# A three-part network on one core: a token mixer whose engines take some hundred pieces per chunk in a written order of their own

## The reference

```python
delta = shifted - x
z = tanh((x + delta * mu_x) @ W_x1.T)                   # 5 x 32 low-rank channels
mus = einsum('blnr,dnr->blnd', z, W_x2) + x_bias        # five mixes of 256 channels
r = (x + delta * r_mu) @ W_r.T                          # k, v, g alike, w by two matmuls
w = tanh((x + delta * w_mu) @ A_w.T) @ B_w.T + b_w
# per token: o = q (S + u k v), S = exp(-exp(w)) S + k v
o = (o - mean) / sqrt(var + EPS) * gn_weight + gn_bias
y = (o * silu(g)) @ W_o.T
```

## Time and profile before

| | us |
|---|---|
| median of 3 executions (3580.39 to 3586.51) | 3586.17 |
| the profiled execution | 3589.31 |
| its span in the trace | 3587.5 |
| mixer, first 16 chunks' work to its last residual add | 0 to 874.9 |
| PE, DVE, ACT, POOL busy over the whole span | 92%, 69%, 56%, 22% |
| granted TensorE clock, whole span | 0.935 |

### The profile page before, as it was taken

How to read it: one execution, slowest core, us unless ns; L and a number is a source line. 1 busy time by engine, 2 the same in 40 slices (tenths; PEclk the granted TensorE clock), 3 DMA queues, 4 the chain that set the end, 5 groups by cost and what they waited for, 6 DMA issues and landing times. The chain is left out here.

```text
span 3587.5 us, 77850 instructions
## 1 busy us (share of the span) xinstructions
PE 3299.5 (92%) x31396; PEld 1943.6 (54%) x31396; DVE 2487.4 (69%) x4742; ACT 2006.8 (56%) x2999; POOL 775.6 (22%) x888
## 2 busy tenths in 40 slices
PE   7999999995899939999999999999999999987998
PEld 3555556554677814444444444444444444436777
DVE  5766676664777717777868778677687776826776
ACT  2444444442555503666766667666666666675555
POOL 2444444442222210102011011020110201011222
PEclk8898888886899966999999999999999999998999
DMA  1000000002111142121212222131212212102111
GB/s 49 14 25 13 25 25 25 14 14 67 61 48 48 36 95 38 27 43 46 43 30 59 41 48 42 23 66 25 58 34 38 54 35 39 38 13 85 48 54 36
DMA packets 110294, 145.48 MB, mean 41 GB/s; under 512 B 21616, under 2 KB 94208, under 8 KB 109152
## 3 DMA queue, kind: packets, MB, share of 16 engines
q1 hardware_dynamic: 109168, 137.69, 16.3%
q0 software_dynamic: 768, 2.82, 0.4%
HBM read 53.89 MB, written 38.24 MB: 26 GB/s over the span
## 5 line engine op out<-in xcount | busy, mean ns | idle before, releaser
L1795 DVE TENSOR_REDUCE b_half_max<-banks 128x1 f32<-128x512 f32 x2048 | 1314.6, 685 | 443.5 <-PE banks L1520 262.3
L1746 ACT ACTIVATE b_p_t<-banks 128x1024 f32<-128x1024 f32 x1024 | 1045.8, 1024 | 398.3 <-PE banks L1520 256.7
L1576 PE MATMUL banks<-b_k_stack,b_q_stack 62*128 62x512 f32 x2048 | 828.5, 477 | 34.1 <-issue 17.8
L1637 PE MATMUL banks<-b_q_stack,b_k_stack 64*128 64x512 f32 x2048 | 851.5, 469 | 0.0
L1592 PE MATMUL banks<-b_p_t,b_v 128*17 128x256 f32 x8192 | 640.9, 385 | 25.1 <-ACT b_pv L1715 24.5
L1637 PEld LDWEIGHTS banks<-b_q_stack,b_k_stack 64*128 64x128 f32 x2048 | 343.0, 185 | 432.1 <-issue 416.7
L1520 PE MATMUL banks<-b_tables,b_halves 64*128 64x128 bf16 x4096 | 437.0, 224 | 0.0
L1576 PEld LDWEIGHTS banks<-b_k_stack,b_q_stack 62*128 62x128 f32 x2048 | 337.6, 188 | 68.5 <-issue 24.9
L1125 ACT ACTIVATE ffn_relu<-banks,ffn_scale_fc 128x512 f32<-128x512 f32 x256 | 176.0, 687 | 234.1 <-PE banks L1057 234.0
L1070 PE MATMUL banks<-ffn_proj_t,ffn_r_hi 128*128 128x256 f32 x1024 | 262.2, 289 | 8.7 <-DVE ffn_r_lo L1251 8.7
L1592 PEld LDWEIGHTS banks<-b_p_t,b_v 128*17 128x17 f32 x8192 | 136.0, 95 | 225.1 <-issue 77.0
(11 more groups left out here) (232 smaller groups left out, 4978.2 us busy)
## 6 DMA issues: line engine op xcount, KB each, us to landing
ffn_x<-x SPq DMA_DIRECT2D x32, 512.0 KB, 3.9
b_q_stack<-b_qk_hi SPq DMA_DIRECT2D x256, 64.0 KB
b_k_stack<-b_qk_hi SPq DMA_DIRECT2D x256, 64.0 KB
a_x<-hidden_states SPq DMA_DIRECT2D x16, 512.0 KB, 4.1
x<-a_x SPq DMA_DIRECT2D x16, 512.0 KB, 2.9
x<-ffn_x SPq DMA_DIRECT2D x16, 512.0 KB, 2.8
b_x<-x SPq DMA_DIRECT2D x8, 1024.0 KB, 5.8
b_k_stack<-b_qk_lo SPq DMA_DIRECT2D x128, 64.0 KB
```

The costliest lines, as they stand in the source:

```text
L1576: last = pe.matmul(m, q_stack[rows, slot, qb * P:(qb + 1) * P], k_stack[rows, slot, half * BANK:(half + 1) * BANK], start=True, stop=not h ...
L1637: last = pe.matmul(out, k_stack[stack, slot, kb * P:(kb + 1) * P], q_stack[stack, slot, half * BANK:(half + 1) * BANK], start=True, stop=n ...
L1746: act.activation(p_t[use % P_BUFS][:, :, :], scores[use % 2], ACT.Exp, scale=slopes()[pair][0]).then_inc(p_made, 1)
L1795: dve.tensor_reduce(half_max[:, (pair + rg * PAIRS) * QB + qb, half:half + 1], misc.at["max", g, turn], axis=AX.X, op=ALU.max, negate=True ...
```

## The change

The four generators of each engine are cut into named pieces (`turn`, `mix_in`, `low`, `pair_products`, `carry_over`, `output`, `project_out`, `level` and so on), and `schedule` goes. Each engine has a list of its own for one turn, written out, with the chunk that each piece works on: PE's reaches from chunk `c - 2` to `c + 2`, DVE's to `c + 3`. `advance` is cut in `carry_over` and `output`, which can stand apart; the last block's `output` and the output projections of a chunk come one turn later than before, and `keys` now comes before `queries`. ACT's `queries`, `keys` and `take_values` get a wait of their own for the buffers (`used_up`), and the tree's first level one for `q`. No instruction, tile or buffer count of the computation changes.

```diff
@@ -221,8 +221,10 @@
         MIXED = ((0, 0), (1, 0), (0, 1), (1, 1), (2, 0), (3, 0), (2, 1), (3, 1), (4, 0), (4, 1))
         SCALED = [max(i for i, (j, _) in enumerate(MIXED) if j == mix) + 1 for mix in range(MIXES)]
         FIRSTS, WEIGHTS = 4, 6 + 1 + 6 + 4 + 2 * KT
-        NORMALIZE, PREPARE, RECUR, FINISH = 7, 14, 8, 12
         Z_ROWS = (P, 2 * LOWRANK)
+
+
+        TURNS = range(-3, CHUNKS + 3)
         ring = Ring([banks[:, i, :] for i in range(6)], (zeroed, 1))
         mix = lambda j: mixes[j % (MIXES - 1)]
 
@@ -232,6 +234,10 @@
         def mix_free(c, j):
 
             return ((g_ready, 2 * c), (r_ready, c), (k_ready, c), (v_ready, 2 * c), (low_ready, c + 1))[j]
+
+        def on(c, piece, *which):
+            if 0 <= c < CHUNKS:
+                piece(c, *which)
 
...
-        def schedule(recur, finish, prepare, normalize):
-            for c in range(-2, CHUNKS + 1):
-                side_by_side(*([(RECUR, recur(c), 1)] if 0 <= c < CHUNKS else []),
-                             *([(FINISH, finish(c - 1), 1)] if c > 0 else []),
-                             *([(PREPARE, prepare(c + 1), 1)] if 0 <= c + 1 < CHUNKS else []),
-                             *([(NORMALIZE, normalize(c + 2), 1)] if c + 2 < CHUNKS else []))
-                yield c
-
...
+            def carry_over(c, i):
+                t, keys = CT * c + i, k_tok[(CT * c + i) % 2]
+                b, (used, n) = ring.take(("kv", c, i), (state_made, t + 1))
+                pe.wait_ge(used, n)
+                pe.wait_ge(v_made, 2 * c + i // 2 + 1)
+                pe.wait_ge(k_tok_made, t + 1)
+                for h in range(HEADS_A):
+                    r = h * HK
+                    last = pe.matmul(b[r:r + HK, 0:HV], keys[:, r:r + HK], v[c % 2][:, i, h * HV:(h + 1) * HV],
+                                     start=True, stop=True, tile_position=(0, r))
+                last.then_inc(kv_ready, 1)
+
+            def output(c, i):
+                tok, t = i * P, CT * c + i
+                fresh, weights = t % QB == 0, pair[t % 2]
+                b, (used, n) = ring.take(("o", c, i), (o_made, t + 1))
+                pe.wait_ge(used, n)
+                if not fresh:
+                    pe.wait_ge(state_spread, t)
+                    pe.matmul(b[:, 0:VD], q_up[c % 2][TREE][:, tok:tok + P], spread_state[t % 2][:, :, :].rearrange("p h n -> p (h n)"),
+                              start=True, stop=False)
+                pe.wait_ge(near_placed, t + 1)
+                for h in range(HEADS_A):
+                    last = pe.matmul(b[:, h * HV:(h + 1) * HV], weights[:, h, :], v[c % 2][:, i, h * HV:(h + 1) * HV],
+                                     start=fresh, stop=fresh or h == HEADS_A - 1)
+                last.then_inc(o_ready, 1)
+
...
+            for c in TURNS:
+                on(c + 1, mix_in, 0)
+                on(c + 1, mix_in, 2)
+                on(c, pair_products, 0)
+                on(c - 1, output, 3)
+                on(c - 2, project_out, 0)
+                on(c - 2, project_out, 1)
+                on(c - 2, project_out, 2)
+                on(c + 1, mix_in, 4)
+                on(c + 1, mix_in, 6)
+                on(c + 1, low)
+                on(c, pair_products, 1)
+                on(c - 2, project_out, 3)
+                on(c + 1, decays)
+                on(c + 1, mix_in, 8)
+                on(c + 1, keys)
+                on(c, carry_over, 0)
+                on(c, pair_products, 2)
+                on(c, carry_over, 1)
+                on(c, output, 0)
+                on(c + 1, queries)
+                on(c + 2, turn, 0)
+                on(c, output, 1)
+                on(c + 2, turn, 1)
+                on(c + 1, values, 0)
+                on(c, pair_products, 3)
+                on(c, carry_over, 2)
+                on(c + 1, gates, 0)
+                on(c + 1, values, 1)
+                on(c - 1, turn_out)
+                on(c, output, 2)
+                on(c + 1, gates, 1)
+                on(c + 2, low_rank, 0)
+                on(c + 2, low_rank, 1)
+                on(c, carry_over, 3)
...
+            def decays(c):
+                dec = decay[c % 2]
                 act.wait_ge(w_ready, c + 1)
                 used_up(c - 2)
...
+            for c in TURNS:
+                on(c + 1, take_low_rank, 1)
+                on(c, level, 6)
+                on(c, pair_products, 0)
+                on(c - 1, output, 3)
+                on(c + 1, low)
+                on(c - 1, squares)
+                on(c, pair_products, 1)
+                on(c + 1, keys)
+                on(c + 1, decays)
+                on(c, pair_products, 2)
+                on(c, output, 0)
+                on(c + 1, queries)
+                on(c + 1, level, 0)
+                on(c, output, 1)
+                on(c + 2, take_turned, 0)
+                on(c + 1, level, 1)
+                on(c + 1, take_values, 0)
+                on(c + 1, level, 2)
+                on(c + 2, take_turned, 1)
+                on(c + 1, level, 3)
+                on(c, pair_products, 3)
+                on(c - 1, take_o_t, 0)
+                on(c + 1, take_values, 1)
+                on(c + 1, take_gates, 0)
+                on(c + 1, level, 4)
+                on(c + 1, take_gates, 1)
+                on(c, output, 2)
+                on(c + 1, level, 5)
+                on(c + 2, take_low_rank, 0)
+                on(c - 1, take_o_t, 1)
...
+            for c in TURNS:
+                on(c, pair_products, 0)
+                on(c - 2, project_out, 0)
+                on(c + 1, add_x)
+                on(c - 2, project_out, 1)
+                on(c - 2, project_out, 2)
+                on(c + 1, mix_in, 4)
+                on(c + 1, mix_in, 6)
+                on(c, pair_products, 1)
+                on(c - 2, project_out, 3)
+                on(c - 1, power)
+                on(c + 1, mix_in, 8)
+                on(c, carry_over, 0)
+                on(c + 2, normalize)
+                on(c, pair_products, 2)
+                on(c, carry_over, 1)
+                on(c - 1, scale)
+                on(c + 1, level, 0)
+                on(c + 1, level, 1)
+                on(c + 1, level, 2)
+                on(c, pair_products, 3)
+                on(c + 2, difference)
+                on(c, carry_over, 2)
+                on(c + 2, first_mix)
+                on(c + 1, level, 3)
+                on(c + 1, gates, 0)
+                on(c + 1, level, 4)
+                on(c + 3, moments_of)
+                on(c + 1, level, 5)
+                on(c + 1, level, 6)
+                on(c + 1, gates, 1)
+                on(c, carry_over, 3)
+                on(c + 2, mix_in, 0)
+                on(c + 2, mix_in, 2)
...
+            for c in TURNS:
+                on(c, level, 4)
+                on(c, level, 5)
+                on(c - 1, carry_over, 2)
+                on(c, level, 6)
+                on(c - 1, carry_over, 3)
+                on(c - 2, gate_out)
+                on(c + 2, root)
+                on(c + 1, add_x, 2)
+                on(c + 1, add_x, 3)
+                on(c + 2, carry_token)
+                on(c - 1, root_out)
+                on(c, carry_over, 0)
+                on(c + 1, level, 0)
+                on(c + 1, add_x, 4)
+                on(c + 1, level, 1)
+                on(c + 1, level, 2)
+                on(c, carry_over, 1)
+                on(c + 1, level, 3)
```

More of the change, by code:

```diff
@@ new lines, in values @@
+            def values(c, h):
+                b, (used, n) = ring.take(("v", c, h), (v_made, 2 * c + h + 1))
+                pe.wait_ge(used, n)
+                pe.wait_ge(*mixed(c, 3))
+                for i in range(2):
+                    tok = (2 * h + i) * P
+                    out = b[:, i * VD:(i + 1) * VD]
+                    pe.matmul(out, mix(3)[:, 0, tok:tok + P], w_v[:, 0, :], start=True, stop=False)
+                    last = pe.matmul(out, mix(3)[:, 1, tok:tok + P], w_v[:, 1, :], start=False, stop=True)
+                last.then_inc(v_ready, 1)
@@ L400, in recur @@
[L400 to L412 removed]
+                                out, moving = products[at:at + BLOCK, h, LEVEL[l]:LEVEL[l + 1]], qs[l][r, now]
@@ new lines, in pair_products @@
+                                if l:
+                                    out, moving = out.rearrange("p (n m) -> p n m", m=1 << l), upper(moving, l)
+                                pe.matmul(out, ks[l][r, now], moving, start=True, stop=True, tile_position=(h * HK, at))
+                    for at in range(0, P, BLOCK):
+                        late = tok + BLOCK + at // 2
+                        for h in heads:
+                            r = slice(h * HK, (h + 1) * HK)
+                            last = pe.matmul(products[at:at + BLOCK, h, LEVEL[NEARBY]:], ks[NEARBY][r, tok:tok + BLOCK],
+                                             qs[NEARBY][r, late:late + BLOCK // 2], start=True, stop=True, tile_position=(h * HK, at))
```

(43 more changed lines are left out.)

651 lines of the change are left out of this document (220 added, 431 removed).

## The result

The changed kernel takes **3489.67 us** (median of four runs, 3481.44 to 3500.58); before takes 3584.2 in the runs beside it. The ratio is 0.9739, with a 95% interval of 0.9703 to 0.9775: 94 us less. The forecast was 3490. Two of the four runs are near 3481, two near 3499.

A forecast was written before the change was run, and what follows sets the result against it. PE was taken to bound the kernel. Per chunk, 42.0 us of full-clock work + 0.5 of new wait + 2.0 of lost clock = 44.5 in place of 50.9; 96 us less over 15 chunks gave 3490 us, range 3450 to 3565.

The forecast's parts named there:

- The wait between pair products 0 and 1: PE's wait for `a_pair`, 1.6 us per chunk, goes because over 7 us of other work now stands there.
- The new wait: At the turn's start `mix_in` waits for the low-rank tanh: 0.5 us per chunk, counted in full.
- The other engines: DVE, ACT and POOL work, tree levels and `add_x` cost nothing while PE needs over 42 us per chunk.
- the ring: PE's waits for banks at `mix_in` 4 to 7 and `low`: taken as 0, bounds 0 and 1 us per chunk.
- Four `mix_in` as one issue: At the turn's start, four matmuls on two row groups run at once, in one issue of 1.06 us.
- rival B: `mix_in` goes two by two, 2.1 us, with a clock fall each chunk: 47.6 us per chunk, 3537 us; chance 0.23.
- The 42.0 us of PE work at full clock: PE's work per chunk, from the old 50.9 us less 6.4 of half clock and 2.5 idle.
- The clock: Falls to half speed every second chunk, 8 us each: 4 us per chunk, costing 2 us; bounds 0 and 6.4.
- Ends: First and last turns: 1 us more, up to 8 us more and up to 4 us less; taken as 0.
- Rival A: The clock never falls in the mixer's turns: 42.5 us per chunk, 126 us less, 3460 us; chance 0.30.
- Rival C: The clock falls twice a turn, at the start and pair products 2: 52.5 us per chunk, 3610 us; chance 0.07.

The follow-up runs named there:

- control: The changed kernel again, unaltered, measured beside the follow-ups: 3483.15 us.
- gates_last: Changed kernel with the second gate projection moved behind the two low-rank projections, covering the tanh wait at the turn's start: 3468.01 us.
- thin: Changed kernel with only four `mix_in` matmuls between pair products 0 and 1, as before the change; the rest behind pair products 1: 3552.96 us.
- fill: Changed kernel plus one full-depth matmul per turn, result overwritten, ahead of the tanh wait at the turn's start: 3475.79 us.
- dense: Changed kernel with only two output projections between pair products 0 and 1, all `mix_in` there moved behind pair products 1: 3554.71 us.
- best: Changed kernel with the edits of gates_last, tail and rows4b together, and `project_out` 3 ahead of `low`: 3463.73 us.
- tail: Changed kernel with chunk 14's output turned, gated and projected in turn 15 in place of a turn later: 3479.28 us.
- rows4b: Changed kernel with `mix_in` matmuls resequenced onto four distinct row groups, and PE, DVE and ACT lists reordered to avoid two waits: 3480.04 us.
- apart: As best, but with `low` and `project_out` 3 behind pair products 1: 3452.89 us.

## Why the prediction was right

The way and most of the steps were right. That the time was met within a microsecond is luck: the same kernel took 3483 us in control, and the two profiled executions differ by 107.3 us where the sum said 96. The turns came out shorter than forecast (43.5 us over the 15 chunks, with 44.5 forecast) and the ends longer.

*The wait between pair products 0 and 1* went, as said. *The new wait* for tanh is 0.43 us per turn, with 0.5 forecast. *The other engines* cost nothing: no wait of PE for another tile shows in the middle, and the ring cost nothing. DVE is busy for 339.11 of 441.70 us, 77% (78% forecast). These were the steps worked out from durations.

*Four `mix_in` as one issue* was wrong. Here rival B was right, and the rule of the Trainium skill ("TensorE: Matmul & The Clock Gate", Part 3: Packing small matmuls) that I had weighed and set aside: the trace agrees with it, with 1.92 us for four on two row groups, and 1.16 and 1.14 for four on four. The row that I trusted shows eight records in flight; that is not eight at work.

*The 42.0 us of PE work at full clock* measured 42.7 in gates_last. The packing is only a part of the reason. An estimate from the groups' times at full clock, each from its start to the start of the next (`low` taken from the changed kernel), gives 42.7 for the kernel before as well: the ten `mix_in` went from 4.35 to 4.9 us per chunk, and transposes and block outputs took about as much less. What was too low was the start of the sum: half of the busy time at half clock was taken off, and pair products shrink by less, from 3.71 us (419.31 to 423.02 in the kernel before) to 2.15. I had called the halving a little too kind and put no number on it.

*The clock* was forecast with a fall in every second turn of 8 us, 4 us cold per chunk and 2.0 us lost. Measured were four falls in ten turns, 2.4 us cold, and about 1.0 lost (44.2 less 42.7 less 0.43). The place (turn's start) and the frequency were about right, the length was not: 6.0 us in the mean and not 8. That the three projections behind the block output cut it short is my reading; without them there (thin) it was 10.24 us in every turn. So 0.7 us too little for PE's work and 1.0 too much for the clock nearly cancel: 42.7 + 0.43 + 1.0 = 44.2, against 42.0 + 0.5 + 2.0 = 44.5.

*Ends*: taken as 0, measured 5.4 us more: the first pair products begin 2.4 us earlier, not 1 us later, and the last stretch is 7.8 us longer, mostly by work that was shifted there from the first turns.

Rival B is half right: two by two, but no fall in each turn, so 44.2 in the middle and not 47.6. Rival A was nearer to the mechanism than I allowed (0.30): with the 0.43 us filled the clock stays up for ten turns (fill, gates_last). The rule of the Trainium skill beside it ("TensorE: Matmul & The Clock Gate", Why this matters for your kernels) names idle gaps, and by it the clock was to stay up here. It did not: it fell four times behind gaps of 0.43 us. That filling this gap ends the falls speaks for gaps having a part; that one of 1.1 us did nothing in dense, and that best's clock fell with none, shows that they are not all. Rival C's fall at pair products 2 does occur, at 19 to 20 us into a turn, once each in ten turns of control, tail and rows4b and twice in apart.

What the gain is made of, per turn in the middle, 51.2 to 44.2: idle time fell from 2.6 to 0.43 us, and PE's busy time from 48.6 to 43.7 with the same matmuls. With 42.7 us of full-clock work on both sides (for before the estimate above), the clock's cost fell from 5.9 to 1.0. So about 4.9 of the 7.0 us are the clock and 2.2 the waits.

## What to carry over

Where PE is the bound, keep its thin matmuls (few rows or few columns) apart with dense ones between them, fill a wait with dense work that is ready (gates_last), and let no long run of thin work follow a wait that stays; here one order of the same instructions costs 70 us more than another. The 32-row matmuls here ran four at once on four row groups and two at once on two. Before moving anything for that, list what else the moved result feeds: a packing that saved 0.8 us brought two waits of 4.2 us together.

## What was not expected

- With one more matmul per turn the clock stayed up through ten turns, and without it it fell in four: the added work left the kernel at 3475.8 us in place of 3483.2 (intervals of the ratios 0.9682 to 0.9711 and 0.9705 to 0.9730, which overlap a little).
- A fall can last far longer in one turn than in the next of the same kernel: 20.48 us in two turns of dense, 3.4 or 6.8 in three others, and never over 6.8 in ten turns of the changed kernel.
- The same program has a different number of falls in each run: 3481 to 3501 us for the changed kernel, 3537 to 3563 for dense. Where in the turn they lie is mostly steady (the start, or behind pair products 2), in which turn is not.
